# Feed-forward weights at earlier steps of the last body, quantising between the gated products, and three products and the last conversion's third chunk on GpSimd

## The chip, the cores and the metric

One core of one Trainium2 chip runs the kernel. The metric is the device time of one execution in microseconds, the median over several runs. The engines are TensorE (PE, with its weight loads as PEld), VectorE (DVE), ScalarE (ACT), GpSimd (POOL) and SyncE (SP, which here only issues DMAs). They run their own instruction streams in order and meet through semaphores.

## What is computed

```
x   32 x 64 x 128 latents, ctx 32 x 1601 x 128, mask 32 x 1601
x = x + cross_attention(ctx, layernorm(x), mask)    # 16 heads of 64, softmax over 1601 + 64 keys, layernorm of the output
x = x + self_attention(layernorm(x))                # 16 heads of 8, with slopes * (key - query)
x = x + ffn(layernorm(x))
ffn(x):  xq = fake_quant(x, clip_x)                 # one scale: sigmoid(clip) * max|x| / 127 over the whole tensor
         h  = silu(xq @ q(w_gate).T) * (xq @ q(w_up).T)          # 352 wide; q(w): per row scale max|w| / 127, rounded
         return fake_quant(h, clip_down) @ q(w_down).T           # again one scale over the whole tensor
```

The kernel looks at the mask (whether any of the first 1201 keys is in play) and runs one of two plans, over all 1601 context keys or over the last 400. The run profiled here takes the second, WINDOW.

## The kernel before, in words

**Bodies and steps.** The 32 batches go in 16 pairs. A body is one pair: 16 steps, eight for each of its two batches (k = 0, 1; t = s % 8). Body 0 and 1 are written out, 2 to 14 are a hardware loop, body 15 is the last. In a step TensorE makes a tile of scores (three f16 products of 512 columns), ScalarE takes the exponential twice (L1084 as f16, L1075 as f32), GpSimd subtracts the one from the other (L845, `low_probs`), and TensorE multiplies high and low parts with the values two steps later (L1421, `values`). Other work is hung on steps by a table: a pair's own tail starts in its body and goes on in the next (`background`, with s + 16). The tables name the step: ST1, YN, ST2 are the output product of the cross attention with the division by the denominators, M0/P0/X1 its layernorm, M1/P1/XH the next layernorm, XHT a transpose, QKV the self attention's projections, KEXP the keys spread over heads by a mask (GpSimd, L905), VBLK the values, SC the scores (L1516), ALIBI and SMAX slopes and maximum (VectorE), SHIFT, EXP, PT, PV, CX (context divided, VectorE L1858, L1860), CXT, WO, X2/P2, XF the normalised input of the feed-forward part. Within a step each engine does its own work in the order: attention, tail of the pair, feed-forward weights.

**Feed-forward weights** (`ffn_weights`, in body 15 only, for k = 1 and by t). SP loads them early in the body (`load_ffn`, L689 to L691). VectorE finds the scales (L1743 to L1750), rounds each of three chunks of gate, of up, and the down weights with three instructions (L1707, L1708, L1709, each waiting for the one before), and makes a diagonal of the down scales (L1758). TensorE transposes them into two banks (L1285, L1289, L1292), and VectorE copies them out (L1763 to L1768).

**The drain.** Behind body 15 stand the last two value tiles, then `drain_pairs`: the tails of pair 14 (table BEFORE_LAST) and 15 (LAST_PAIR) side by side, 22 steps. At step 0 GpSimd spreads the keys of pair 14, TensorE makes its scores, then for pair 15 the sum of denominators (L1462) and the output product (L1480, L1490). VectorE takes ALIBI and SMAX of pair 14, then the reciprocals of pair 15's denominators (L1873) and the products with them (L1882).

**The feed-forward part.** After the largest |x| is known, four groups of 512 tokens are quantised: raised by a constant (L2010 on VectorE for groups 0, 1; L1200 on ScalarE for 2, 3), then L2013 and L2014 on VectorE. Then 12 products, m = 3 * group + chunk: TensorE makes gate and up into banks (L1615, L1616), ScalarE SiLU into one of two buffers (L1207), VectorE up times SiLU (L2029), and behind each group the largest |h| (L2022, in the last group in two pieces). Then the scale of h through TensorE (L1619, L1621), and for four groups j: h to int8, all three chunks (L2044); int8 to bf16, chunks 0 and 1 on ScalarE (L1211), chunk 2 on VectorE (L2046); 12 products (L1628); scaling (L2052) and the residual added, on GpSimd for j = 0, 1 (L966), on VectorE for 2, 3 (L2055); a DMA out.

## Time and profile before

| | us |
|---|---|
| median of 3 runs (848.68 to 850.6) | 848.82 |
| the profiled execution | 846.89 |
| its span | 845.1 |
| busy: PE, DVE, ACT, POOL | 762.6, 606.2, 586.6, 519.2 |
| granted TensorE clock, mean | 0.964 of full |

The span is what the profile's times refer to, from its start. In the 40 slices of the page (21 us each) PE shows 9 tenths in slices 5 to 36 and then 7, 7, 4, 3 (the last four: 7743), with a granted clock of 9 tenths up to slice 37 and then 6, 6, 5. The page's chain that ended last has 65% on PE, 18% on DVE, 6% issue, 5% ACT, 2% POOL.

### The profile page before, as it was taken

Reading aid. Unit: us, or ns where it says so; the run is one execution under the profiler, and the core shown is the slowest. Engines: PE = TensorE matmul, PEld = TensorE weight load, DVE = VectorE, ACT = ScalarE, POOL = GpSimd, SP = SyncE. Lnnn points to the kernel's source line nnn. Section 1 sums busy time; section 2 is a strip of 40 time slices with the busy share of each in tenths; the row PEclk is TensorE's granted clock in tenths of the full one; section 3 lists DMA queues with packets and bytes.
Section 4 is the critical chain, followed back from the end, with each engine's and each line's share of the span. In section 5 each row is a group of like instructions: output and inputs, shape, how many; then the busy total and the mean of one; then the engine's idle time right before and its main releaser. Section 6 shows DMA issues by size and latency. Waiting matters only on the chain.

```text
span 845.1 us, 22525 instructions
## 1 busy us (share of the span) xinstructions
PE 762.6 (90%) x7062; PEld 419.5 (50%) x7063; DVE 606.2 (72%) x1515; ACT 586.6 (69%) x1018; POOL 519.2 (61%) x660
## 2 busy tenths in 40 slices
PE   5698999999999999999999999999999999997743
PEld 3343544545464555545454545555455546455412
DVE  5777676676768686876777686878767676757587
ACT  5487677868777676868686776768686867673242
POOL 3366676766767676666667676757666676764101
PEclk9799999999999999999999999999999999999665
DMA  6212222121212212021212121121112121200001
GB/s 191 56 44 79 74 66 50 46 69 39 59 53 55 57 53 56 21 55 43 68 41 66 43 57 55 53 59 32 44 41 68 43 68 38 73 14 17 4 0 50
DMA packets 95821, 44.42 MB, mean 53 GB/s; under 512 B 66500, under 2 KB 87848, under 8 KB 95656
## 3 DMA queue, kind: packets, MB, share of 16 engines
q1 hardware_dynamic: 95728, 43.93, 18.9%
q8 instruction: 17, 0.28, 0.1%
q14 instruction: 20, 0.16, 0.1%
q10 hardware_dynamic: 56, 0.05, 0.0%
HBM read 24.20 MB, written 3.34 MB: 33 GB/s over the span
## 4 chain that ended last, share of the span: by engine, by line
PE 65%; DVE 18%; issue 6%; ACT 5%; DVEq 2%; POOL 2%; DMA 1%; ACTq 0%; SPq 0%; POOLq 0%
PE bank L1421 14%; PE bank L1480 7%; PE bank L1384 6%; PE bank L1339 5%; PE bank L1388 5%; PE bank L1386 5%; PE bank L1356 4%; PE bank L1497 3%; PE bank L1541 3%; DVE xf_all L1851 3%; DVE mx L1822 3%; PE bank L1526 2%; PE bank L1516 2%; PE bank L1355 2%; DVE st L1779 1%
## 5 line engine op out<-in xcount | busy, mean ns | idle before, releaser
L845 POOL TENSOR_TENSOR p<-arena,p 128x512 f16<-128x512 f32 x256 | 297.1, 1161 | 167.2 <-ACT arena L1075 166.7
L1084 ACT ACTIVATE p<-bank,maskbias 128x512 f16<-128x512 f32 x224 | 155.1, 692 | 125.6 <-PE bank L1388 124.6
L1421 PE MATMUL bank<-p,xv 128*128 128x512 f16 (+1 forms) x768 | 182.6, 380 | 4.1 <-POOL p L845 2.7
L1822 DVE TENSOR_REDUCE mx<-bank 128x1 f32<-128x464 f32 x256 | 154.1, 634 | 32.3 <-PE bank L1356 31.0
L1075 ACT ACTIVATE arena<-bank,maskbias 128x512 f32<-128x512 f32 x224 | 154.6, 690 | 0.5 <-POOL p L845 0.5
L1818 DVE TENSOR_TENSOR qkl_l<-bank,qkl_h 128x512 f16<-128x512 f32 x64 | 41.1, 686 | 71.2 <-ACT qkl_h L1064 71.1
L1421 PEld LDWEIGHTS bank<-p,xv 128*128 128x128 f16 (+1 forms) x768 | 57.2, 97 | 70.0 <-issue 22.6
L1384 PE MATMUL bank<-qkc_h,xtT_h 128*128 128x512 f16 (+1 forms) x256 | 86.9, 389 | 0.0
L1388 PE MATMUL bank<-qkc_h,xtT_l 128*128 128x512 f16 (+1 forms) x256 | 85.0, 379 | 0.0
L1386 PE MATMUL bank<-qkc_l,xtT_h 128*128 128x512 f16 (+1 forms) x256 | 85.0, 379 | 0.0
L1356 PE MATMUL bank<-xtT_h,qkc_h 128*128 128x400 f16 x256 | 79.7, 338 | 0.0
L1480 PE MATMUL bank<-arena,wvF 128*64 128x128 f32 x1024 | 69.3, 278 | 0.0
L1339 PE MATMUL bank<-arena,wk_h 64*128 64x128 f16 x1024 | 50.1, 217 | 15.5 <-DVE arena L1809 14.9
L1480 PEld LDWEIGHTS bank<-arena,wvF 128*64 128x64 f32 x1024 | 54.7, 136 | 14.5 <-issue 13.1
L1814 DVE SCALAR_TENSOR_TENSOR arena<-bank,ident,arena 128x512 f16<-128x512 f32 x60 | 42.0, 738 | 26.6 <-ACT arena L1061 26.6
L1339 PEld LDWEIGHTS bank<-arena,wk_h 64*128 64x128 f16 x1024 | 37.0, 94 | 42.1 <-DVE arena L1809 22.1
L1355 PE MATMUL bank<-ltT,qkl_h 128*128 128x64 f16 x256 | 50.7, 198 | 4.9 <-DVE qkl_l L1818 3.2
L1355 PEld LDWEIGHTS bank<-ltT,qkl_h 128*128 128x128 f16 x256 | 24.9, 97 | 59.0 <-DVE mx L1822 26.3
L1788 DVE TENSOR_SCALAR raw<-raw,mv,rstd 128x128 f32<-128x128 f32 x128 | 51.1, 458 | 1.9 <-POOL rstd L854 1.7
L1061 ACT ACTIVATE arena<-bank,ident 128x512 f16<-128x512 f32 x60 | 37.9, 684 | 16.3 <-PE bank L1339 16.3
L1339 PE MATMUL bank<-arena,wk_l 64*128 64x128 f16 x512 | 46.1, 216 | 0.0
L1084 ACT ACTIVATE p<-bank,zrow 128x512 f16<-128x512 f32 x32 | 22.0, 687 | 26.5 <-PE bank L1392 26.5
(267 smaller groups left out, 1548.8 us busy)
## 6 DMA issues: line engine op xcount, KB each, us to landing
arena<-den_dram SPq DMA_DIRECT2D x62, 128.0 KB, 3.2
qkc_h<-arena SPq DMA_DIRECT2D x30, 256.0 KB, 2.4
qkc_l<-arena SPq DMA_DIRECT2D x30, 256.0 KB, 2.5
raw<-in_ctx SPq DMA_DIRECT2D x32, 192.0 KB, 2.4
lt<-lt_dram SPq DMA_DIRECT2D x60, 32.0 KB, 2.1
arena<-in_L_xattn_Wkv SPq DMA_DIRECT2D x1, 1024.0 KB, 6.8
raw<-in_ctx SPq DMA_DIRECT2D x64, 8.0 KB, 2.0
ltT_dram<-x_all SPq DMA_DIRECT2D x4, 256.0 KB, 3.0
```

What stands on the lines that cost most here:

```text
L845: g.tensor_tensor(p_halves[0:r, slot, 1, :], p_all[0:r, (plan.halves_made(0, k, t) - 1) % 2, :], p_halves[0:r, slot, 0, :], ALU.subtract). ...
L1075: a.activation(p_all[0:r, (plan.halves_made(0, k, t) - 1) % 2, :], sbank[t % SRING][0:r, :], ACT.Exp, bias=bias).then_inc(s_probs_ready, 1)
L1084: a.activation(p_halves[0:r, slot, 0, :], sbank[t % SRING][0:r, :], ACT.Exp, bias=bias)
L1339: op = mm(by_batch(both[odd])[:, :, to], w[rws, cl, c, :], q[rws, c, :].rearrange("p (k t) -> p k t", k=2), start=first, stop=final)
L1355: mm(bk[:, rest:rest + M], qkl_h[:, par, col], ltT[:, par, 0, :], start=True, stop=True)
L1356: op = mm(bk[:, 0:rest], qkc_h[:, par, col], xtT_h[:, par, 512 * part:plan.KEYS], start=True, stop=True)
L1384: op = mm(dst, keys_h, q_h[:, col], start=True, stop=False)
L1386: op = mm(dst, keys_h, q_l[:, col], start=False, stop=False)
L1388: op = mm(dst, keys_l, q_h[:, col], start=False, stop=tile > 0)
L1421: op = mm(bk[:, :], halves_of[at, row, :], p_halves[at, slot, prob, :], start=tile < 2 and n == 0, stop=last and n == 2)
L1480: op = mm((one, two)[q // 2][E * odd:E * odd + E, (c % 4) * P:(c % 4) * P + P], wvF[:, cl, head:head + E], z[:, :, col:col + M], start=cl ...
L1822: v.tensor_reduce(mx[:, hq_tile, part:part + 1], bk[:, 0:width], AX.X, ALU.max).then_inc(s_jobs_taken, 1)
```

## The change

- The feed-forward weights go by the step s of the body, not by t within k = 1: scales at s = 7 (before 10), rounding at 8 and 9 (11, 12), TensorE's transposes and the copies at 10, 11, 12, 13 (12, 13, 14, 15).
- For WINDOW the keys of pair 14 are spread before the last `low_probs`, and its scores are made between the last two value tiles.
- Group 1 is raised on ScalarE. Groups 0 and 1 are quantised before the products, group 2 behind product 2, group 3 behind product 5. The maximum of a group comes behind the first product of the next.
- Products 1, 4 and 7 are made on GpSimd: ScalarE writes SiLU and, scaled, up into SBUF buffers of their own.
- The cast of chunk 2 to bf16 is on GpSimd, in front of its two residual additions.

```diff
--- before.py
+++ after.py
@@ -53,7 +53,7 @@
...
 ALIBI_AT = 16
-FFN = dict(scales=2, round=[3, 4], fw=[4, 5], fwd=[6], wd=[7])
+FFN = dict(scales=7, round=[8, 9], fw=[10, 11], fwd=[12], wd=[13])
 
@@ -201,7 +201,7 @@
...
 BEFORE_LAST = Drain(False, dict(
-    NEVER, KEXP=0, X1B=1, SC=0, ALIBI=[1, 1], SMAX=1, SHIFT=2, EXP=2, PT=[5, 5], PT_OUT=[5, 5], PV=6, CX=8, CXT=9, CXT_OUT=9, WO=10, X2=11, P2=12, XF=14))
+    NEVER, X1B=1, SC=-2, ALIBI=[1, 1], SMAX=1, SHIFT=2, EXP=2, PT=[5, 5], PT_OUT=[5, 5], PV=6, CX=8, CXT=9, CXT_OUT=9, WO=10, X2=11, P2=12, XF=14))
 LAST_PAIR = Drain(True, dict(
@@ -348,6 +348,8 @@
...
         s_xqT_ready = es.enter_context(nc.semaphore("xqT_ready"))
+        s_up_copied = es.enter_context(nc.semaphore("up_copied"))
+        s_h_pool = es.enter_context(nc.semaphore("h_pool"))
         s_xtT_hi = es.enter_context(nc.semaphore("xtT_hi"))
@@ -444,6 +446,7 @@
...
         h8 = words(12288, 1536).bitcast(I8).rearrange("p (c t) -> p c t", c=3)
+        pool_sil, pool_up = (raw[:, :, :, :].rearrange("p a c d -> p (a c d)")[:, at:at + 512] for at in (2048, 2560))
         yout = raw[:, :, :, :].rearrange("p a c d -> p (a c d)")[:, 0:2048].rearrange("p (a b) -> p a b", a=4)
@@ -597,6 +600,16 @@
...
 
+        POOL_TILES = (1, 4, 7)
+
+        def on_pool(m):
+
+            return sum(n <= m for n in POOL_TILES)
+
+        def on_dve(m):
+
+            return m + 1 - on_pool(m)
+
         block = es.enter_context(nc.Block())
@@ -879,6 +892,14 @@
...
 
+            def spread_keys(p):
+
+                pool.wait_ge(s_qk_ready, p + 1)
+                if happened(2 * p):
+                    pool.wait_ge(s_self_scores, 2 * p)
+                g.tensor_tensor(kexp, kT[:, :].rearrange("p (k m) -> p k m", k=2).unsqueeze(2).to_broadcast([P, 2, AH // 2, M]),
+                                halfmask[:, :].unsqueeze(1).unsqueeze(3).to_broadcast([P, 2, AH // 2, M]), ALU.mult).then_inc(s_kexp_ready, 1)
+
             def tail(plan, p, s):
@@ -899,11 +920,7 @@
...
                 if s == at["KEXP"] and not plan.own:
-                    pool.wait_ge(s_qk_ready, p + 1)
-                    if happened(2 * p):
-                        pool.wait_ge(s_self_scores, 2 * p)
-                    g.tensor_tensor(kexp, kT[:, :].rearrange("p (k m) -> p k m", k=2).unsqueeze(2).to_broadcast([P, 2, AH // 2, M]),
-                                    halfmask[:, :].unsqueeze(1).unsqueeze(3).to_broadcast([P, 2, AH // 2, M]), ALU.mult).then_inc(s_kexp_ready, 1)
+                    spread_keys(p)
                 if s == at["SHIFT"]:
@@ -950,6 +967,8 @@
...
                 body(PAIRS - 1, 2, True)
+                if plan is WINDOW:
+                    spread_keys(PAIRS - 2)
                 low_probs(plan, PAIRS - 1, 1, plan.STEPS - 1)
@@ -961,6 +980,13 @@
...
             drain_pairs(None, tail, 14, DRAIN_STEPS)
+            for m in POOL_TILES:
+                pool.wait_ge(s_up_copied, on_pool(m))
+                g.tensor_tensor(hT[:, m % 3, 512 * (m // 3):512 * (m // 3) + 512], pool_up, pool_sil, ALU.mult).then_inc(s_h_pool, 1)
+            for j in range(4):
+                pool.wait_ge(s_h8_ready, j + 1)
+                part = slice(512 * j, 512 * j + 512)
+                g.tensor_copy(hq[:, 2, part], h8[:, 2, part]).then_inc(s_hq_ready, 1)
             for j in range(2):
@@ -1196,15 +1222,24 @@
...
             act.wait_ge(s_xscale_ready, 1)
-            for m in (2, 3):
-                a.activation(xq32[:, 512 * m:512 * m + 512], abank[m - 2][:, :], ACT.Identity, scale=fst[:, 3:4], bias=magic[:, :]).then_inc(s_x_raised, 1)
+            for m in (1, 2, 3):
+                act.wait_ge(s_groups_out, 2)
+                src = xfT[:, 512:1024] if m == 1 else abank[m - 2][:, :]
+                a.activation(xq32[:, 512 * m:512 * m + 512], src, ACT.Identity, scale=fst[:, 3:4], bias=magic[:, :]).then_inc(s_x_raised, 1)
             act.wait_ge(s_sgu_ready, 1)
...
                 act.wait_ge(s_gate_made, m + 1)
-                if happened(m - 1):
-                    act.wait_ge(s_h_ready, m - 1)
-                a.activation(sil[:, m % 2, :], bank[2 + m % 3][:, :], ACT.Silu, scale=sgu[:, 0, c:c + 1]).then_inc(s_silu_ready, 1)
+                if m in POOL_TILES:
+                    if on_pool(m) > 1:
+                        act.wait_ge(s_h_pool, on_pool(m) - 1)
+                    a.activation(pool_sil, bank[2 + m % 3][:, :], ACT.Silu, scale=sgu[:, 0, c:c + 1]).then_inc(s_silu_ready, 1)
+                    act.wait_ge(s_up_made, m + 1)
+                    a.activation(pool_up, up_bank[m % 3][:, :], ACT.Identity, scale=sgu[:, 1, c:c + 1]).then_inc(s_up_copied, 1)
+                else:
+                    if on_dve(m) > 2:
+                        act.wait_ge(s_h_ready, on_dve(m) - 2)
+                    a.activation(sil[:, on_dve(m) % 2, :], bank[2 + m % 3][:, :], ACT.Silu, scale=sgu[:, 0, c:c + 1]).then_inc(s_silu_ready, 1)
             for j in range(4):
@@ -1572,8 +1607,8 @@
...
                             late_weights(s + 2 * plan.STEPS * since, since)
-                        if last and k == 1:
-                            ffn_weights(plan, t)
+                        if last:
+                            ffn_weights(plan, s - plan.STEPS + WINDOW.STEPS)
 
@@ -1583,6 +1618,8 @@
...
                     values(plan, PAIRS - 1, 1, t)
+                    if plan is WINDOW and t == plan.STEPS - LAG:
+                        drained(BEFORE_LAST, PAIRS - 2, BEFORE_LAST.at["SC"])
 
@@ -1610,8 +1647,10 @@
...
                     pe.wait_ge(s_silu_ready, m - 2)
-                if happened(m - 2):
-                    pe.wait_ge(s_h_ready, m - 2)
+                if m - 3 in POOL_TILES:
+                    pe.wait_ge(s_up_copied, on_pool(m - 3))
+                elif m >= 3:
+                    pe.wait_ge(s_h_ready, on_dve(m - 3))
                 mm(bank[2 + m % 3][:, :], fwT[:, 0, rows], xqT[:, 512 * tg:512 * tg + 512], start=True, stop=True).then_inc(s_gate_made, 1)
@@ -1976,8 +2015,8 @@
...
                             late_weights(s + 2 * plan.STEPS * since)
-                        if last and k == 1:
-                            ffn_weights(t)
+                        if last:
+                            ffn_weights(s - plan.STEPS + WINDOW.STEPS)
 
@@ -2004,31 +2043,39 @@
...
             dve.wait_ge(s_groups_out, 2)
-            for m in range(4):
+
+            def quantised(m):
+
                 part = slice(512 * m, 512 * m + 512)
-                if m < 2:
+                if m == 0:
                     link(v.tensor_scalar(xq32[:, part], xfT[:, part], fst[:, 3:4], MAGIC, ALU.mult, ALU.add))
                 else:
-                    dve.wait_ge(s_x_raised, m - 1)
+                    dve.wait_ge(s_x_raised, m)
                 link(v.tensor_scalar(xqT[:, part], xq32[:, part], MAGIC, QMAX, ALU.subtract, ALU.min))
                 v.tensor_scalar(xqT[:, part], xqT[:, part], -QMAX - 1.0, None, ALU.max).then_inc(s_xqT_ready, 1)
-                if m == 0:
-                    v.tensor_scalar(sgu[:, :, :], fw_s[:, :, :], fst[:, 2:3], None, ALU.mult).then_inc(s_sgu_ready, 1)
+
+            quantised(0)
+            v.tensor_scalar(sgu[:, :, :], fw_s[:, :, :], fst[:, 2:3], None, ALU.mult).then_inc(s_sgu_ready, 1)
+            quantised(1)
             dve.wait_ge(s_sgu_ready, 1)
...
 
-                dve.wait_ge(s_h_ready, 3 * tg + c1)
+                dve.wait_ge(s_h_ready, on_dve(3 * tg + c1 - 1))
+                if on_pool(3 * tg + c1 - 1):
+                    dve.wait_ge(s_h_pool, on_pool(3 * tg + c1 - 1))
                 return v.tensor_reduce(hmax[:, 3 * tg + c0:3 * tg + c1], hT[:, c0:c1, 512 * tg:512 * tg + 512], AX.X, ALU.max, apply_absolute_value=True)
 
-            for m in range(12):
+            for m in (m for m in range(12) if m not in POOL_TILES):
                 tg, c = divmod(m, 3)
...
                 dve.wait_ge(s_silu_ready, m + 1)
-                v.scalar_tensor_tensor(h, up_bank[m % 3][:, :], sgu[:, 1, c:c + 1], sil[:, m % 2, :], ALU.mult, ALU.mult).then_inc(s_h_ready, 1)
-                if tg < 3 and c == 2:
-                    largest(tg, 0, 3)
+                v.scalar_tensor_tensor(h, up_bank[m % 3][:, :], sgu[:, 1, c:c + 1], sil[:, on_dve(m) % 2, :], ALU.mult, ALU.mult).then_inc(s_h_ready, 1)
+                if tg < 2 and c == 2:
+                    quantised(tg + 2)
+                if tg > 0 and c == 0:
+                    largest(tg - 1, 0, 3)
                 if tg == 3 and c >= 1:
@@ -2042,8 +2089,6 @@
...
                 v.tensor_scalar(h8[:, :, part], hT[:, :, part], fst[:, 7:8], None, ALU.mult).then_inc(s_h8_ready, 1)
-                dve.wait_ge(s_h8_ready, j + 1)
-                v.tensor_copy(hq[:, 2, part], h8[:, 2, part]).then_inc(s_hq_ready, 1)
                 if j == 0:
```

## Rows read from the trace of the kernel before

**Rows 1.** Timeline of VectorE in the last body: start, duration, engine, line, operation, shapes, idle before.
```profile
745.15 0.67 DVE L1882 TENSOR_TENSOR arena<-bank,arena 128x512 f32<-128x512 f32 x1
...
749.93 0.30 DVE L1846 BATCH_NORM_STATS2 sst<-bank 128x6 f32<-128x128 f32 x1 [4.11 <-PE bank L1497]
...
752.30 0.06 DVE L1743 MEMSET fw_s<- 128x6 f32 x1
...
754.25 0.12 DVE L1750 RECIPROCAL fwd_s<-fwd_s 128x1 f32<-128x1 f32 x1
...
757.93 1.11 DVE L1709 TENSOR_SCALAR fwq<-arena 128x128 bf16<-128x128 f32 x1
...
758.97 0.27 DVE L1707 TENSOR_SCALAR arena<-arena,fw_i 96x128 f32<-96x128 f32 x1
...
765.00 0.28 DVE L1758 TENSOR_SCALAR arena<-ident,fwd_s 128x128 f32<-128x128 f32 x1
```

**Rows 2.** Waits from 755 to 765 us: who waited for whom, us, times, longest.
```profile
PE bank L1285 <- DVE fwq L1709: 3.5, 2, 2.3
```

**Rows 3.** Timeline of SP's DMA queue, 728 to 746 us.
```profile
734.96 0.42 SPq L691 DMA_DIRECT2D arena<-in_L_ffn_w_down  x1
```

**Rows 4.** DMA issues by line, 728 to 746 us: count, KB, median us to landing.
```profile
arena<-in_L_ffn_w_down SPq DMA_DIRECT2D x1, 176.0 KB, 2.4
```

**Rows 5.** Timelines of VectorE and GpSimd, earlier in the last body.
```profile
723.09 1.96 DVE L1788 TENSOR_SCALAR raw<-raw,mv,rstd 128x128 f32<-128x128 f32 x4
...
723.67 1.30 POOL L845 TENSOR_TENSOR p<-arena,p 128x512 f16<-128x512 f32 x1 [0.37 <-ACT arena L1075]
...
738.70 0.68 DVE L1921 SCALAR_TENSOR_TENSOR arena<-bank,alibi 128x512 f32<-128x512 f32 x1
```

**Rows 6.** Timeline of GpSimd in the last body.
```profile
747.43 1.16 POOL L845 TENSOR_TENSOR p<-arena,p 128x512 f16<-128x512 f32 x1
...
748.96 1.17 POOL L845 TENSOR_TENSOR p<-arena,p 128x512 f16<-128x512 f32 x1
...
752.53 1.15 POOL L845 TENSOR_TENSOR p<-arena,p 128x512 f16<-128x512 f32 x1 [1.15 <-ACT arena L1075]
...
769.11 1.15 POOL L845 TENSOR_TENSOR p<-arena,p 128x512 f16<-128x512 f32 x1 [0.67 <-ACT arena L1075]
```

**Rows 7.** Timelines of GpSimd, VectorE and TensorE in the drain.
```profile
770.22 1.90 POOL L905 TENSOR_TENSOR arena<-kT,halfmask 128x1024 f32<-128x1024 f32 x1
...
775.80 1.75 DVE L1873 RECIPROCAL arena<-bank 128x256 f32<-128x256 f32 x1
...
780.92 1.16 PE L1490 MATMUL bank<-wout_sb,arena 128*128 128x128 f32 x8 [0.32 <-DVE arena L1882]
```

**Rows 8.** Instructions on the arena, VectorE: count, duration ns min/median/max, start, form.
```profile
L2022 DVE TENSOR_REDUCE hmax<-arena x5: 686/1753/1755, 813.7 to 826.9; 128x3 f32<-128x1536 f32 x3, 128x2 f32<-128x1024 f32 x1, 128x1 f32<-128x512 f32 x1
...
L2013 DVE TENSOR_SCALAR arena<-arena x4: 419/424/427, 808.0 to 810.7; 128x512 bf16<-128x512 f32 x4
```

**Rows 9.** Timeline of the gated products.
```profile
809.59 1.48 ACT L1207 ACTIVATE arena<-bank,sgu 128x512 f32<-128x512 f32 x2 [0.60 <-remote]
...
811.32 1.40 DVE L2029 SCALAR_TENSOR_TENSOR arena<-bank,sgu,arena 128x512 f32<-128x512 f32 x2
```

**Rows 10.** Timeline of the last conversion and the output.
```profile
829.67 1.28 DVE L2044 TENSOR_SCALAR arena<-arena,fst 128x1536 int8<-128x1536 f32 x1
...
830.99 0.43 DVE L2046 CAST arena<-arena 128x512 bf16<-128x512 int8 x1
...
839.86 1.04 DVE L2055 TENSOR_TENSOR raw<-raw,x_all 128x512 f32<-128x512 f32 x1
```

**Rows 11.** Lines L873 and L966 of GpSimd: count, duration ns min/median/max.
```profile
L873 POOL CAST xv<-raw x32: 602/608/612, 28.1 to 732.4; 128x508 f16<-128x508 f32 x32
...
L966 POOL TENSOR_TENSOR raw<-raw,x_all x2: 1266/1502/1737, 837.4 to 838.6; 128x512 f32<-128x512 f32 x2
```

**Rows 12.** Windows: us, busy us of PE, PEld, DVE, ACT, POOL, granted clock, DMA share, GB/s.
```profile
788.00:790.00 2.00, 1.63 (x11) 1.01 (x7) 1.85 (x6) 0.46 (x2) 0.00 (x0) 0.50 0.00 0
```

## The prediction

> **What bounds the kernel now.** I read the page's slices first: TensorE is busy nine tenths up to the last three of forty, so only what TensorE waits for counts there, and behind the loop every engine's chain counts. Then the chain of waits from 700 us on, then the timeline of each engine over it. The reader is to see four stretches.
> The last body ends badly: VectorE idles 4.1 us before 749.93, then makes the feed-forward weights from 752.30 to 765.28 [rows 1], and TensorE stands 3.5 us for them [rows 2]. In the drain the chain runs through VectorE: scores of pair 14, their maximum, the reciprocals at 775.80 [rows 7]. In the gated products VectorE is busy nearly throughout (products 0.70 us in a row, the maximum of a group 1.75) [rows 8, 9]. In the last conversion it alternates 1.28 and 0.43 us [rows 10].
>
> **A. Weights made earlier.** Before: scales at step 10, rounding at 11 and 12. After: scales at 7, rounding at 8 and 9, TensorE's transposes at 10, 11, 12, 13. Nothing is added or taken away. The last weight transfer is issued at 734.96 [rows 3] and takes 2.4 us [rows 4]; VectorE comes to step 7's end at 745.80, so the load is no wait, and SP's order is the same.
> What matters is how GpSimd and VectorE exclude each other [rows 5]. Four normalisations (0.33 each alone) take 1.96 us, because a GpSimd subtraction came in between them; that subtraction itself took 1.30 instead of 1.16, since it waited for one of the four. So one waits for the other's instruction, and they alternate. The instruction at 738.70, with one input in PSUM, ran its usual 0.68 beside a subtraction of 738.74 to 739.90. The rounding is of the first kind: 0.23 alone, 1.11 under GpSimd [rows 1].
> The walk: scales 745.80 to 747.87 (2.07, from 752.30 to 754.37). A chunk's three instructions take 0.79 alone (758.97 to 759.76 in the chain), three chunks 2.4. At 747.87 GpSimd is in a subtraction until 748.59, then has an addition and another subtraction [rows 6]: VectorE's first instruction waits to 748.55, its second to 749.2, its third to 750.55, and the rest end at 752.35. Behind them stands the moments step that ran at 749.93; it now ends at 752.9. For it waits GpSimd (two small instructions, 0.85), and behind those the subtraction of 752.53, now at 754.0 to 755.1: TensorE needs it at about 756.5, so this is covered.
> Second round: 2.4, with the down weights and the diagonal 1.3 (763.94 to 765.28), and two subtractions between, 2.1 in all: 752.95 to 758.7. Behind it stand X1 and its moments (1.35), a copy (0.3) and the self context CX (0.55): CX is ready at 761.0. TensorE, no longer held for the weights, is at the transpose of CX at 759.0 and waits 2.0 to 2.1; the second transposes wait 0.2. Removed 3.5, added 2.3: **-1.2 us**. Ends: with no rounding blocked, CX is 4.1 earlier and the whole 3.5 is gained (-3.5); with two or three more blocked, at 0.9 each, +1.0 and more.
>
> **B. Spread keys and self scores of pair 14 ahead.** GpSimd makes the spread keys (1.90) before the last subtraction instead of behind it [rows 7]; its wait is for the keys' copy by ScalarE at step 14, which is there. It had 0.67 idle before that subtraction [rows 6], so the subtraction, TensorE's last values and ScalarE's copies of them come 1.2 later against the rest, but the self scores now fill TensorE's hole. The sum of denominators, which used to start behind keys and scores, keeps its place (minus A). VectorE's scores and maximum are over before it, so the reciprocals of 775.80 start with the denominators, 0.7 earlier. TensorE then no longer waits 0.32 at 780.92. **-0.3 us**; ends -0.8 (all of VectorE's) and +0.8 (the last subtraction's delay, if it is not hidden).
>
> **C. Gated products.** Raising group 1 moves from VectorE (0.48) to ScalarE (0.70, in the place where it was idle until 809.59): SiLU 0 starts 0.1 later. Quantising groups 2 and 3 (0.43 and 0.29 each, 0.74 with the waits) moves from in front of product 0 to behind products 2 and 5. Products 1, 4, 7 leave VectorE (2.1), and ScalarE gets three copies of up (0.70 each). On GpSimd a product is one of 1.16 to 1.27 [rows 5, 11].
> The walk: SiLU 0 ends 810.4, product 0 at 811.2. ScalarE then does SiLU 1, the copy of up 1, SiLU 2, to 812.6, and VectorE is idle 1.4. From there it has 8 products (5.6), two quantisations (1.5), three maxima of 1.68 and those of 1.17 and 0.72, which is 14.05: 826.65. GpSimd's products fall at 811.9, 814.7 and 818.0, the quantisations at 813.4 and 817.2: no overlap. Each product of GpSimd is over more than 1.5 us before the maximum that waits for it. ScalarE's fifteen are 10.5 in 16, TensorE at half clock 0.86 a step: neither is late. Before it was 827.6. **-0.9 us**; ends -2.3 (no hole) and +0.5 (a quantisation behind a product of GpSimd, 1.2, and the next SiLU with it).
>
> **D. Last conversion.** Removed: four casts of 0.43 on VectorE [rows 10]. Added: four on GpSimd. No row shows int8 to bf16 there; f32 to f16 of 508 columns is 0.61 [rows 11]. Take 0.6; ends 0.43 and 1.2. With t from 829.67: VectorE's h8 0 ends 1.28, the row for the scales 1.5. Now GpSimd reads and writes SBUF while VectorE wants it. h8 handles 1536 columns in 1.28 us, 0.83 ns each, as fast as only the kind that was blocked above: 512 columns in 0.42 [rows 8]; the maximum over 1536 takes 1.75, 1.1 ns each, and that kind was never blocked. So I take it as blocked. GpSimd's cast 0 gets 1.5 to 2.1; h8 1 2.1 to 3.3 and h8 2, already queued, to 4.5; cast 1 to 5.1; h8 3 to 6.3; casts 2 and 3 to 7.4. TensorE needs ScalarE's and GpSimd's part: its four blocks (1.44, 1.29 in a row) start 2.45, 5.1, 6.9, 8.2 and end 9.6. GpSimd's additions now start behind its casts, at 7.4, 1.26 each, to 9.95; VectorE's addition 2, two SBUF inputs, waits for them (such a wait is in the 1.04 of 839.86), ends 10.5, then scaling 3 and addition 3 to 11.8. Before, 840.90 is 11.2. **+0.6 us**. If VectorE's h8 always wins the order, the same GpSimd additions end at 9.95 again, so the sum is the same. Ends: without exclusion -1.8 (below), with casts of 1.2, +2.3.
> The Trainium skill, "SBUF — State Buffer", section "Who interferes with whom", says that a cast or tensor_scalar in a 2-port mode and a GpSimd instruction shut each other out for the whole instruction, and that the one issued first goes first. By it D is +0.6; if it did not hold for this form, -1.8. No row has GpSimd beside h8.
>
> **Sum.** -1.2 - 0.3 - 0.9 + 0.6 = -1.8. The profiled execution is 846.89 (span 845.1 and 1.8 around it), so it gives 845.1. The median of the runs shown, 848.82, lies 1.9 above that execution, and I forecast in its terms: **847.0 us**. 0.3% is 2.5 us, about what a measurement of this kernel can tell from no change.
>
> **Rivals.**
> 1. GpSimd's cast does not shut out h8. Then h8 ends at 5.2, TensorE at 8.0, VectorE at 9.4: D is -1.8 and the time **844.6**. For it: no row of this pair. Against it: the rate of h8. Chance 0.15.
> 2. The weights vanish from the path: GpSimd's subtractions fall beside VectorE's scales and PSUM instructions, CX comes before 759, A is -3.3: **844.9**. For it: 4.1 us of idle VectorE. Against: GpSimd is busy from 747.43 to 750.1 nearly without a gap [rows 6]. Chance 0.17.
> 3. Slower: the rounding stands in front of moments, X1 and CX, and GpSimd's queue stands behind those. It decides from CX at 761.0 on: each us later is one more for TensorE. Four more blocked instructions (0.9 to 1.1, 4.3 in all) put CX at 765.3; A is +3.1, B still -0.3, C -0.9, D +0.6: **851.3**. For it: three of seven chunks were blocked by about 0.9 before. Against: GpSimd has but four subtractions under the whole stretch, and the walk has them all. Chance 0.11.
> 4. The clock. TensorE's granted clock is 0.50 of full from 788 on [rows 12], that is 1.2 instead of 2.4 GHz, after a stretch in which TensorE had short holes. If it falls some 3 us earlier against the work, about 1.5 us of matmuls take twice as long: **848.5**. Chance 0.12.
>
> **Chances.** The forecast 0.45. Its own spread puts 0.06 below -2.5 and 0.01 above +2.5. Faster: 0.15 + 0.17 + 0.06 = 0.38; slower 0.11 + 0.01 = 0.12; same 0.50. The range takes in rivals 1, 2 and 4 and the ends of B and C: 844.4 to 849.6. Left out are rival 3, and the cases in which rivals 1 and 2 come together.
>
> **What would show it.** In the profile after: A, the waits of TensorE for the rounded weights gone, and one of about 2 us for CX in their place; rounding instructions of over 1 us between 748 and 758. B, spread keys in front of the last subtraction, no wait of TensorE for VectorE before the second half of the output product. C, VectorE idle about 1.4 us behind product 0 and not after. D, h8 instructions of 1.7 to 1.9 us in place of 1.28, or GpSimd casts that long; the last addition of VectorE behind GpSimd's. It is wrong if h8 keeps 1.28 beside casts of 0.6, or if TensorE has no wait for CX.

## The result, and the profile after

The changed kernel takes **840.39 us** (median of 4 runs, 839.63 to 840.75); the kernel before took 849.71 beside it (4 runs, 848.68 to 851.55). The ratio is 0.9891, with an interval of 0.9877 to 0.9905: 9.3 us less where 1.8 were forecast, and outside the range. The profiled execution is 840.75, its span 838.9, against 846.89 and 845.1. So 6.1 us lie between the two profiled executions and 9.3 between the medians, and both differences have to be explained.

The page of the changed kernel, against the table of before:

```profile
PE 762.7 (91%) x7063; PEld 420.9 (50%) x7063; DVE 604.0 (72%) x1507; ACT 589.4 (70%) x1022; POOL 527.3 (63%) x667
...
PE   5598999999999999999999999999999999998763
...
PEclk9699999999999999999999999999999999999855
```

TensorE is as busy as before (762.7 against 762.6), GpSimd has 8 us more. The last four slices are 8763 where they were 7743, and the clock has 8 tenths in slice 38, where it had 6, and then 5 and 5 for 6 and 5: the same work, closer together.

**The last body.** VectorE's timeline, where rows 1 had the weights behind 752.30 (everything starts 1.27 later in this execution: the last body's SMAX stands at 745.29, in the trace of before at 744.02):

```profile
749.14 0.81 DVE L1746 TENSOR_SCALAR arena<-arena,fw_i 128x128 f32<-128x128 f32 x1
749.98 0.38 DVE L1747 TENSOR_SCALAR arena<-arena 128x128 f32<-128x128 f32 x1
750.39 1.09 DVE L1748 TENSOR_SCALAR fwq<-arena 128x128 bf16<-128x128 f32 x1
751.40 0.28 DVE L1746 TENSOR_SCALAR arena<-arena,fw_i 128x128 f32<-128x128 f32 x1
...
752.83 0.29 DVE L1885 BATCH_NORM_STATS2 sst<-bank 128x6 f32<-128x128 f32 x1
...
754.29 1.18 DVE L1747 TENSOR_SCALAR arena<-arena 128x128 f32<-128x128 f32 x1
...
757.16 1.18 DVE L1748 TENSOR_SCALAR fwdq<-arena 128x352 bf16<-128x352 f32 x1
...
760.30 0.29 DVE L1899 TENSOR_TENSOR cx<-bank,sden 128x128 f32<-128x128 f32 x1
```

The first rounding instruction starts at 749.14, which is 747.87 in before's time, to the hundredth as walked. Five instructions are blocked by a subtraction of GpSimd (0.81, 0.38, 1.09, 1.18, 1.18). CX is over at 760.59, or 759.3 in before's time; the walk said 761.0. The waits of TensorE from 755 to 765 us, where rows 2 had 3.5 us for the weights:

```profile
PE bank L1580 <- DVE cx L1899: 0.5, 1, 0.5
...
PE bank L1456 <- POOL p L858: 0.2, 1, 0.2
```

**The gated products**, VectorE's timeline (rows 9 before):

```profile
807.34 0.75 DVE L2074 SCALAR_TENSOR_TENSOR arena<-bank,sgu,arena 128x512 f32<-128x512 f32 x1 [0.85 <-ACT arena L1242]
809.26 0.75 DVE L2074 SCALAR_TENSOR_TENSOR arena<-bank,sgu,arena 128x512 f32<-128x512 f32 x1 [1.17 <-ACT arena L1242]
809.92 0.42 DVE L2054 TENSOR_SCALAR arena<-arena 128x512 bf16<-128x512 f32 x1
...
811.25 1.74 DVE L2067 TENSOR_REDUCE hmax<-arena 128x3 f32<-128x1536 f32 x1
```

Product 0 is over 3.9 behind the reciprocal of 804.21, as walked; then the one hole, 1.17 where 1.4 was expected, and none over 0.2 after it.

**The last conversion** (rows 10 before). GpSimd's and TensorE's timelines, and of VectorE the line of h8 by its instructions (durations ns min/median/max):

```profile
826.56 0.61 POOL L989 CAST arena<-arena 128x512 bf16<-128x512 int8 x1 [11.13 <-DVE arena L2091]
828.31 2.99 POOL L989 CAST arena<-arena 128x512 bf16<-128x512 int8 x3 [1.14 <-DVE arena L2091]
831.29 2.50 POOL L992 TENSOR_TENSOR raw<-raw,x_all 128x512 f32<-128x512 f32 x2
...
829.48 4.00 PE L1667 MATMUL bank<-fwdT,arena 128*128 128x128 bf16 x36 [0.32 <-POOL arena L989]
```
```profile
L2091 DVE TENSOR_SCALAR arena<-arena,fst x4: 1265/1274/1530, 825.2 to 829.4; 128x1536 int8<-128x1536 f32 x4
```
```profile
832.97 1.37 DVE L2100 TENSOR_TENSOR raw<-raw,x_all 128x512 f32<-128x512 f32 x1
...
834.97 0.69 DVE L2100 TENSOR_TENSOR raw<-raw,x_all 128x512 f32<-128x512 f32 x1
```

One h8 of four is longer, by 0.25; two casts of four are longer, by 0.45. Neither waits for the whole of the other. The traces of d_only and fill_down (below) have the same lengths in the same places: 1.53 for one h8, 1.06 for two casts. From the first h8, the last block of TensorE ends at 8.3 (walked 9.6), GpSimd's casts at 6.1 (7.4), its additions at 8.6 (9.95), VectorE at 10.45 (11.8; before 11.2). The order of events is the one forecast, each step 1.3 earlier.

### The profile page after: what moved, and what is told of

It is laid out like the page before. It is cut to its first block, busy times and chain, and to the rows that moved or that the text cites. A ratio compares the mean times of both kernels' runs of the same rounds, so it can differ in the third digit from the quotient of the medians.

```text
span 838.9 us, 22529 instructions
## 1 busy us (share of the span) xinstructions
PE 762.7 (91%) x7063; PEld 420.9 (50%) x7063; DVE 604.0 (72%) x1507; ACT 589.4 (70%) x1022; POOL 527.3 (63%) x667
## 4 chain that ended last, share of the span: by engine, by line
PE 66%; DVE 17%; issue 7%; ACT 5%; POOL 2%; DVEq 2%; DMA 1%; ACTq 0%; SPq 0%; POOLq 0%
PE bank L1456 14%; PE bank L1515 8%; PE bank L1419 6%; PE bank L1374 5%; PE bank L1423 5%; PE bank L1421 5%; PE bank L1391 4%; PE bank L1532 3%; PE bank L1576 3%; DVE xf_all L1890 3%; DVE mx L1861 3%; PE bank L1551 2%; PE bank L1561 2%; PE bank L1390 2%; DVE st L1818 1%
## 5 line engine op out<-in xcount | busy, mean ns | idle before, releaser
L1087 ACT ACTIVATE arena<-bank,ident 128x512 f16<-128x512 f32 x60 | 38.0, 684 | 15.8 <-PE bank L1374 15.8
L1118 ACT ACTIVATE arena<-bank 128x512 f32<-128x512 f32 x64 | 38.5, 601 | 3.2 <-PE bank L1456 3.2
```

## The experiments

All in one table. Four stretches are read from VectorE's timeline, as differences of start times: **S1** from SMAX in the last body to the first reciprocal of the drain (line 1873 of before); **S2** to the largest |x|; **S3** from the reciprocal of x's scale to the largest |h|; **S4** from the first h8 to the end of the span. "Low until 783" lists when, in the profiled execution, the granted clock was 0.50 for 3.4 us, and "low from" is where it fell for the first long stretch (10 us and more). Medians and ratios are of all executions of a run, the stretches and the clock of its profiled one.

| run | median (lowest to highest, runs) | ratio, interval | S1 | S2 | S3 | S4 | low until 783 | low from |
|---|---|---|---|---|---|---|---|---|
| before | 846.89 (the profiled execution alone) | | 31.78 | 29.53 | 20.35 | 15.48 | none | 787.7 |
| control | 849.36 (848.29 to 851.48, 12) | 1.0005 [0.9996, 1.0014] | 33.39 | 30.05 | 20.35 | 14.48 | 765.5 | 789.4 |
| a_only | 843.56 (842.98 to 844.35, 6) | 0.9935 [0.9923, 0.9948] | 29.17 | 29.40 | 20.34 | 14.50 | none | 785.3 |
| b_only | 845.48 (844.26 to 848.93, 10) | 0.9961 [0.9949, 0.9974] | 31.97 | 29.25 | 20.34 | 14.47 | 763.6 | 787.5 |
| c_only | 847.39 (846.03 to 848.75, 12) | 0.9976 [0.9968, 0.9985] | 34.53 | 30.97 | 18.71 | 14.51 | 764.5, 774.8 | 788.4 |
| d_only | 848.76 (845.54 to 850.57, 12) | 0.9986 [0.9973, 0.9998] | 34.49 | 31.01 | 20.35 | 13.72 | 764.5, 774.7 | 788.4 |
| ab_only | 843.69 (842.77 to 845.02, 6) | 0.9927 [0.9913, 0.9942] | 28.73 | 30.25 | 20.35 | 14.47 | none | 783.5 |
| no_b | 841.51 (840.99 to 843.01, 6) | 0.9905 [0.9891, 0.9920] | 29.16 | 29.28 | 18.96 | 13.69 | none | 786.0 |
| no_d | 843.77 (840.58 to 844.87, 6) | 0.9928 [0.9911, 0.9944] | 28.72 | 28.20 | 18.97 | 14.48 | none | 789.0 |
| after | 840.39 (839.63 to 840.75, 4) | 0.9891 [0.9877, 0.9905] | 28.74 | 28.23 | 18.97 | 13.72 | none | 790.0 |
| after_again | 840.34 (839.52 to 841.20, 5) | 0.9895 [0.9880, 0.9909] | 28.73 | 27.58 | 18.97 | 13.72 | none | 793.1 |
| fill_w | 845.36 (843.31 to 850.75, 7) | 0.9951 [0.9938, 0.9965] | 32.88 | 31.95 | 20.35 | 14.47 | 773.8 | 787.4 |
| fill_both | 847.16 (845.40 to 849.42, 12) | 0.9964 [0.9950, 0.9979] | 31.76 | 29.36 | 20.34 | 14.49 | none | 788.1 |
| c_front | 847.11 (843.59 to 849.28, 10) | 0.9956 [0.9936, 0.9976] | 34.52 | 30.88 | 17.50 | 14.51 | 765.5, 775.7 | 789.4 |
| fill_ffn | 840.27 (840.00 to 841.45, 5) | 0.9894 [0.9880, 0.9909] | 28.73 | 29.49 | 18.90 | 13.70 | none | 785.6 |
| fill_all | 840.07 (839.97 to 840.96, 5) | 0.9895 [0.9881, 0.9909] | 28.74 | 28.29 | 18.91 | 13.70 | none | 785.7 |
| fill_down | 840.75 (838.72 to 841.72, 6) | 0.9887 [0.9863, 0.9912] | 28.71 | 29.24 | 18.93 | 12.88 | none | 784.5 |
| fill_down_order | 842.23 (840.46 to 842.87, 6) | 0.9900 [0.9876, 0.9925] | 28.71 | 30.66 | 18.91 | 13.71 | none | 783.7 |
| quant_front | 839.88 (837.94 to 840.67, 4) | 0.9881 [0.9862, 0.9899] | 28.72 | 30.31 | 17.51 | 13.72 | none | 783.6 |
| quant_front_fill | 838.53 (838.22 to 840.28, 4) | 0.9877 [0.9860, 0.9893] | 28.72 | 28.11 | 18.03 | 12.85 | none | 790.0 |

### The parts by themselves, and the kernel before again

Control is the kernel before, unchanged. The other three have one part of the diff each.

```diff
# a_only: part A
-FFN = dict(scales=2, round=[3, 4], fw=[4, 5], fwd=[6], wd=[7])
+FFN = dict(scales=7, round=[8, 9], fw=[10, 11], fwd=[12], wd=[13])
# b_only: part B
-    NEVER, KEXP=0, X1B=1, SC=0, ...
+    NEVER, X1B=1, SC=-2, ...
+                    spread_keys(PAIRS - 2)
# c_only: part C
+        POOL_TILES = (1, 4, 7)
+                if tg < 2 and c == 2:
+                    quantised(tg + 2)
```

Expected of control:

> The kernel before, unchanged. Two theories of why the medians differ by 9.3 us while the two profiled executions differ by 6.2. Theory 1: the profiled execution of before (846.9) is just a lucky one, in which the granted clock fell late; then other executions of it have a lower mean clock than 0.964, and the profile of this run, if it is near 849.7, shows the fall to 0.50 well before 787 us. Theory 2: executions of before are slower for another reason (more waits in the loop); then the mean clock is 0.964 and the extra 3 us stand before 700 us.

Expected of a_only:

> Only the weights made at earlier steps (part A). Theory 1, the walk with its sizes: TensorE's 3.5 us of waits for the weights are replaced by a wait of 0.5 for CX, so the last values come 2.7 us earlier and the time falls by 2.5 to 3. Theory 2, the clock: the gain is larger, 4 to 6 us, because with fewer holes in the last body the granted clock stays at 1.00 for longer; then the profile shows its fall later against the work of the drain. My prediction had -1.2 for this part.

Expected of b_only:

> Only the spread keys and self scores of pair 14 ahead (part B). Theory 1, the walk: about -0.3 us, at most -0.8. Theory 2, the clock: the order of TensorE's work around its hole of 1 to 2 us decides when the clock falls; then it is -1 to -3 us, with no wait in the profile that is shorter by as much.

Expected of c_only:

> Only the feed-forward stage's products and quantisation (part C), everything before it as in the kernel before. Theory 1: -1.4 us, as between the two profiles from the reciprocal of the x scale to the maximum of h (20.3 to 19.0 us). Theory 2: the gain needs the clock's rise in the stage; then the time in the stage differs by over 0.5 us between executions with their clock. Nothing before the stage may change.

Control is at 849.36 like the other runs of before, so the median stands, but its profile is not that of before. TensorE's timeline has the same hole (a stretch in which it stands still) for the weights as rows 2; the windows behind it differ. First control, then before (columns as in rows 12):

```profile
764.88 0.32 PE L1285 MATMUL bank<-identb,fwq 128*128 128x128 bf16 x3 [2.31 <-DVE fwq L1709]
```
```profile
766.00:768.00 2.00, 2.00 (x8) 1.26 (x6) 1.17 (x6) 1.26 (x2) 0.54 (x1) 0.50 0.00 0
```
```profile
766.00:768.00 2.00, 2.00 (x19) 1.12 (x18) 1.32 (x8) 1.29 (x4) 1.41 (x3) 1.00 0.00 0
```

It was granted 0.50 of full behind the hole (1.2 GHz) and 1.00 (2.4 GHz) without the fall. The two windows hold partly different matmuls, so their counts (8 and 19) don't compare; the same three value products right behind the hole do, in control and then in before:

```profile
765.88 1.48 PE L1421 MATMUL bank<-p,xv 128*128 128x512 f16 x3
```
```profile
764.97 0.81 PE L1421 MATMUL bank<-p,xv 128*128 128x512 f16 x3
```

c_only shows what that does to single matmuls of 512 columns, 0.63 for 0.38, and a second fall behind the next holes:

```profile
764.45 0.40 PE L1310 MATMUL bank<-identb,fwq 128*128 128x128 bf16 x3 [2.32 <-DVE fwq L1736]
764.66 0.63 PE L1409 MATMUL bank<-qkc_h,xtT_h 128*128 128x512 f16 x1
...
768.88 0.38 PE L1409 MATMUL bank<-qkc_h,xtT_h 128*128 128x512 f16 x1
...
772.27 0.82 PE L1446 MATMUL bank<-p,xv 128*128 128x512 f16 x3 [1.07 <-POOL p L858]
774.18 1.45 PE L1541 MATMUL bank<-arena,qT 64*64 64x512 f32 x8 [1.08 <-issue]
775.56 2.80 PE L1487 MATMUL bank<-arena,sel 128*64 128x512 f32 x6
```

S1 orders the runs that keep the order of before by the number of such falls: none, 31.78; one, 33.39; two, 34.5. A fall costs S1 1.1 to 1.6 us. The mean clock of the twelve executions of control is 0.954 to 0.958; that of the profiled execution of before is 0.964. So the profiled execution was one without these falls, and by their mean clocks most are not. Of the five traces that keep this order and this hole (before, control, c_only, d_only, c_front) four show the fall behind it.

**S2** goes by the clock too. No run but fill_all changes its work, and yet it lies between 27.6 and 31.95. What orders it is how long after the first reciprocal of the drain the clock falls for the long stretch: 9.2 to 10.5 us (fill_w, d_only, c_only, c_front, fill_down_order, quant_front, ab_only) give 31.95 down to 30.25; 11.3 in control gives 30.05; 11.9 to 12.3 (before, fill_ffn, fill_both, a_only, no_b, fill_down, b_only) give 29.5 to 29.2; 15.8 to 16.0 (quant_front_fill, no_d, after) give 28.1 to 28.2; 19.2 in after_again gives 27.58. The one exception, fill_all, has the clock back at 1.00 from 796.0 to 799.4.

**A** alone takes S1 from 31.78 to 29.17, which is 2.6, and the median down by 5.5 (0.0065 of 849.7). The 2.9 between them is about what the falls cost: its profile has none before 785. It has none although TensorE still waits 1.29 and 1.08 us around the last value tile, so a hole of this size is followed by a fall in some executions and not in others; what decides it is open. **B** alone takes 1.4 from S1 against control, both with one fall; its median is 3.3 lower. **C** alone takes 1.64 from S3 and 2.0 from the median.

### Two parts, and all but one

```diff
# ab_only: the diffs of a_only and b_only together
# no_b: the changed kernel with SC and KEXP of before
-    NEVER, X1B=1, SC=-2, ...
+    NEVER, KEXP=0, X1B=1, SC=0, ...
# no_d: the changed kernel with the casts on VectorE; d_only: before with them on GpSimd
-                g.tensor_copy(hq[:, 2, part], h8[:, 2, part]).then_inc(s_hq_ready, 1)
+                dve.wait_ge(s_h8_ready, j + 1)
+                v.tensor_copy(hq[:, 2, part], h8[:, 2, part]).then_inc(s_hq_ready, 1)
# after_again: the changed kernel, unchanged
```

Expected of ab_only:

> Parts A and B together, feed-forward stage as before. If both gain by their own waits (2.7 and 0.4 us) and share what they save of the clock, the sum is less than 5.5 + 3.3: theory 1 (shared clock) gives -6 to -7 us; theory 2 (independent gains) gives -8.8. The profile should show no fall of the clock before 785.

Expected of no_b:

> The changed kernel with part B undone: keys spread behind the last subtraction, scores of pair 14 at step 0 of the drain. Theory 1: with A in place B is worth its waits alone, 0.4 to 0.8 us, so 0.4 to 0.8 slower than the changed kernel. Theory 2: B is worth 3.3 us as it was alone.

Expected of no_d:

> The changed kernel with part D undone: the casts of chunk 2 back on VectorE. My prediction had D at +0.6 (this run 0.6 faster than the changed kernel); by the profile of the changed kernel the stretch from the first h8 to the last addition is 10.45 us against 11.23, and the output's transfers start earlier by 1.0: this run 0.8 to 1.7 us slower than the changed kernel.

Expected of after_again:

> The changed kernel once more, for more executions beside those of its variants. It should lie at 840.4 with a mean clock of 0.965 to 0.971. If some of its executions show 0.961, as four of six of the run without part D did, these will lie 2 to 4 us higher: then D has no part in that difference.

Expected of d_only:

> Only the last conversion (part D). From the first h8 to the end of the span the seven profiles without D have 14.5 us (one has 15.5), the two with it 13.7: so 0.8 us faster than before. My prediction had +0.6. If the run without D (3.4 slower than the changed kernel by the medians) is to be believed instead, this one is 3 us faster.

With A in place **B** is worth 0.44 in S1 (29.17 to 28.73, and 29.16 to 28.74 from the other side), not 1.4, and 1.1 in the median of no_b against the changed kernel. The waits of TensorE between the last body and the sum of denominators tell the two cases apart. First a_only, then the changed kernel:

```profile
767.74 0.82 PE L1421 MATMUL bank<-p,xv 128*128 128x512 f16 x3 [1.29 <-POOL p L845]
769.64 1.09 PE L1516 MATMUL bank<-arena,qT 64*64 64x512 f32 x8 [1.08 <-issue]
```
```profile
769.22 1.09 PE L1551 MATMUL bank<-arena,qT 64*64 64x512 f32 x8 [1.51 <-POOL arena L900]
...
772.05 1.94 PE L1497 MATMUL bank<-arena,sel 128*64 128x512 f32 x8 [0.89 <-ACT arena L1118]
```

They add up to 2.37 and 2.40: with A, TensorE is early enough to wait for the spread keys themselves. Without A they are 2.15 in control (1.07 and 1.08) and 1.16 in b_only (0.27 and 0.89). What is left of B in both cases is VectorE's maximum, which no longer stands between the sum of denominators and the reciprocals: these start 1.98 behind the start of the sum in the changed kernel and 1.97 in b_only, for 2.56 in a_only and 2.55 in control.

**D** is worth 0.76 in S4 from either side (14.48 to 13.72 in no_d against after, and in control against d_only). d_only's median, 1.2 below before, agrees. no_d's does not: 3.4 above after_again. Its six executions lie in two groups, 840.58 and 841.67 at a mean clock of 0.966 and 0.967, and 843.2 to 844.9 at 0.959 to 0.961; the profiled one is of the first. None of the five executions of after_again is below 0.967. Why a cast at the end should go with a lower clock is open, since only one execution has a trace.

The parts don't add up by medians (5.5 + 3.3 + 2.0 + 1.2 = 12.0, against 9.3): A and B each take falls of the clock away, and these can go only once. By stretches they do, if B is counted on top of A: S1, S3 and S4 of the changed kernel are those of ab_only, no_b and d_only to within 0.02. Only C alone is off, with 18.71 in S3 for 18.97; product 6 waits there for TensorE's product of up, which took 0.38 in c_only, at a granted clock of 1.00, and 0.63 in the changed kernel, where it was 0.50 from 813.9 on.

### The holes filled

The same product of TensorE, unused, is put into its waits. Nothing is taken away, and what TensorE waits for doesn't come earlier.

```diff
# fill_w: the kernel before; fill_both: with the last two lines too, four each in front of and
# behind the second of the last value tiles
                     if kind == "fw":
+                        for _ in range((5, 10)[k]):
+                            mm(bk[:, :], wq_h[:, 0:P], wq_h[:, 0:HALF], start=True, stop=True)
                         pe.wait_ge(s_fwq_ready, 1 + k)
...
+                        pe.wait_ge(s_ffn_done, 3)
+                        filler(jbank[0], 4)
```

Expected of fill_w:

> The kernel before, with 5 and 10 extra products of 512 columns on TensorE (1.1 and 2.2 us at full clock) in front of its two waits for the rounded weights; the waits of 1.2 and 2.3 us stay, only they are not idle. The products go to the bank that the transposes then overwrite. Theory 1, the clock follows TensorE's holes: the fall to 0.50 that control shows at 765.5 us is gone, and the time falls by 1.5 to 2 us although work was added. Theory 2, the clock does not depend on these holes: no change, or up to 0.3 us slower, and the fall at 765 stays.

Expected of fill_both:

> The kernel before, with extra products of TensorE in its two waits for the weights, as before, and eight more behind the last body, in the wait in front of the last value tile. Theory: the time of the usual execution of the kernel before, 849.7, is its work plus two falls of the granted clock to 0.50 for 3.4 us, one behind the hole for the weights and one behind the hole of the last values; with both holes filled it is 843.5 to 845.5, every execution at a mean clock of 0.966 or more, and none near 850. From the maximum of pair 14's scores to the first reciprocal it keeps some 32 us, since nothing of VectorE's order is changed. Rival: the second fall is not from that hole; then as with the first hole alone, 845.4 in the median and single executions of 848 to 851.

fill_w does 15 products more than before and is **4.2 us faster** (ratio 0.9951, interval clear of 1). The work and its order are the same but for the added products, and the mean clock is 0.966 to 0.968 in six of the seven executions, for 0.956 to 0.959 in those of before beside them: the clock behind the hole costs time. Its profiled execution is its slowest, 850.75, and shows that the gain is not in every one: with the first hole filled, the next one gives a fall. TensorE's timeline, and a window behind it:

```profile
771.61 0.82 PE L1423 MATMUL bank<-p,xv 128*128 128x512 f16 x3 [1.07 <-POOL p L845]
773.51 1.77 PE L1518 MATMUL bank<-arena,qT 64*64 64x512 f32 x8 [1.08 <-issue]
```
```profile
774.00:777.00 3.00, 3.00 (x14) 0.56 (x8) 1.68 (x3) 0.00 (x0) 0.46 (x1) 0.50 0.00 0
```

In fill_both the same waits are 0.21 and 0.17 and the window has the full clock:

```profile
770.58 0.82 PE L1423 MATMUL bank<-p,xv 128*128 128x512 f16 x3 [0.21 <-POOL p L845]
772.43 1.09 PE L1523 MATMUL bank<-arena,qT 64*64 64x512 f32 x8 [0.17 <-POOL arena L905]
```
```profile
774.00:777.00 3.00, 3.00 (x42) 2.14 (x40) 2.97 (x4) 0.00 (x0) 1.05 (x2) 1.00 0.02 5
```

Its profiled execution, 845.93 with S1 at 31.76, is the profiled execution of before without its late output: there the span ends 4.2 behind VectorE's last instruction (840.90), in control 3.25 (843.75 to 847.0), and 846.89 less 1.0 is 845.9. But my theory's number failed. The median is 847.16, not 843.5 to 845.5, and no better than fill_w's (the intervals overlap); five of twelve executions still have a clock of 0.958 to 0.962 and take 846.2 to 849.4. The holes explain most of the distance between 845.9 and 849.7, not all of it: where the remaining falls sit isn't known, the place of the long fall in S2 was left to chance, and what the eight further products cost by themselves wasn't measured.

### Part C taken apart

```diff
# c_front: c_only with the quantising in front; quant_front: the same in the changed kernel
             quantised(1)
+            quantised(2)
+            quantised(3)
...
-                if tg < 2 and c == 2:
-                    quantised(tg + 2)
```

Expected of c_front:

> The kernel before with part C alone, but groups 2 and 3 quantised in front of product 0, as before. If VectorE bounds the stretch, the two quantisations (0.74 each with their waits) come in front of product 0 again, where TensorE and ScalarE have work to get ahead with: the hole of 1.17 behind product 0 shrinks, and of the 1.5 in front only what the hole does not give back is lost, 0.3 to 1.5, so from the scale of x to the last maximum of h 19.0 to 20.2 instead of 18.7 with C whole and 20.35 without it. Rival: the interleaving alone carries C, and the three products on GpSimd give nothing: 20.2 to 20.4.

Expected of quant_front:

> The changed kernel with one part of its change taken back: groups 2 and 3 are quantised in front of product 0, not behind products 2 and 5. Theory: in front, the two quantisations cost 0.4, since VectorE waits 0.85 there for the first SiLU anyway, and behind products they cost 0.66 each on the engine that bounds; so from the scale of x to the last maximum of h it is 17.7 instead of 18.97, and the time 839.1. Rival: with the weights earlier and the cast on GpSimd the stretch is bounded otherwise than in the run with part C alone: 18.5 to 19.0, and 840.3 as before.

Both sides of c_front's expectation missed. S3 is 17.50, below c_only's 18.71: what ScalarE and GpSimd take over (the raising of group 1, the copies, the three products) and the later maxima give 2.85 together (from 20.35), and quantising between the products **costs 1.2**. VectorE's timeline of c_only, then of c_front:

```profile
814.87 0.75 DVE L2061 SCALAR_TENSOR_TENSOR arena<-bank,sgu,arena 128x512 f32<-128x512 f32 x1 [0.85 <-ACT arena L1232]
816.79 0.75 DVE L2061 SCALAR_TENSOR_TENSOR arena<-bank,sgu,arena 128x512 f32<-128x512 f32 x1 [1.17 <-ACT arena L1232]
```
```profile
816.00 0.74 DVE L2063 SCALAR_TENSOR_TENSOR arena<-bank,sgu,arena 128x512 f32<-128x512 f32 x1
817.53 1.51 DVE L2063 SCALAR_TENSOR_TENSOR arena<-bank,sgu,arena 128x512 f32<-128x512 f32 x2 [0.80 <-ACT arena L1232]
```

In c_only VectorE idles 0.85 in front of product 0 and 1.17 behind it, in c_front only 0.80 behind it. In front, the two quantisations (0.66 each, 1.32 together) fill 1.22 of idle time; between the products, where VectorE has no gap, they fill none. quant_front repeats it in the changed kernel, where it costs 1.5 (18.97 to 17.51). Its median is 0.5 under after_again, not 1.2; in its profile the clock falls at 783.6 already, and S2 is 30.31 against 28.23 and 27.58.

### The clock in the feed-forward part

```diff
# fill_ffn, on the changed kernel
+            filler(bank[3], 3)                  # in front of the products
+                    filler(abank[1], 1)         # in front of each product from the fourth on
+            filler(abank[1], 8)                 # while the largest |h| is found
+            filler(abank[1], 5)                 # behind it
# fill_all: as fill_ffn, and six more in three waits of the drain
# fill_down: as fill_ffn, with 17 and 11 for 8 and 5
# fill_down_order: as fill_down, VectorE's scalings 2 and 3 ahead of its additions 2 and 3
# quant_front_fill: fill_down with the quantising in front
```

Expected of fill_ffn:

> The changed kernel with extra products on TensorE where it waits in the feed-forward stage: 3 in front of the first product, 1 in front of each from product 3, 8 before the maximum of h, 5 before the last conversion's blocks. Theory 1, the clock follows the holes here too: it stands at 1.00 in the last conversion, its four blocks take 0.7 instead of 1.3 us, and the time falls by 1 to 2 us. Theory 2: the clock stays at 0.50; then the extra products are in the way and the time is 0 to 1 us longer.

Expected of fill_all:

> The same, and with extra products in the drain: 2 before the second transposes of probabilities, 1 before the transpose of the context, 3 before the last transpose of the normalised input. Theory 1: the clock also rises before 810, and another 1 to 2 us go. Theory 2: no rise, 0.3 to 1.5 us slower than the changed kernel.

Expected of fill_down:

> The changed kernel with more extra products in TensorE's waits of the feed-forward part: one behind each of the products from the fourth on, 17 while the maximum of h is found, 11 in front of the last conversion's products. Theory: the granted clock is 1.00 in the last conversion too, its blocks take 0.7 us instead of 1.3, and from the first h8 to the end it is 12.8 to 13.2 instead of 13.7, the time 839.5. Rival: the clock is still 0.50 there, or VectorE and GpSimd set the end anyway, and the time is that of the changed kernel, 840.3, or up to 1 more.

Expected of fill_down_order:

> As the run before it, and VectorE scales chunks 2 and 3 before it adds chunks 2 and 3, so that its first addition does not hold up the last scaling behind GpSimd's additions. Theory: the last addition comes 0.2 to 0.5 earlier than without this, whatever the clock does. Rival: addition 2 waits for GpSimd as before and nothing stood behind it that mattered: no difference, within 0.1 in the profile.

Expected of quant_front_fill:

> The run before this with the extra products of TensorE in its waits of the feed-forward part, by which the granted clock was 1.00 in the last conversion. Theory: the two gains add up: 17.7 for the stretch of the gated products, 12.9 from the first h8 to the end, 838.0 in the median. Rival: what the clock gives there is lost in single executions, as in fill_down, whose median was no better than the changed kernel: 839 to 840.

fill_ffn and fill_all hold the clock at 1.00 from 809.4 to 823.1, and it moves S3 by 0.07, with the added products in TensorE's way: VectorE bounds nearly all of it (product 6, above, was the one that waited for the clock). The last conversion is at 0.50 again in both, and the time is that of the changed kernel. fill_all's products in the drain did bring the clock back, to 1.00 from 796.0 to 799.4, and its S2 is 28.29 where fill_ffn, with the fall at the same place, has 29.49; its median is only 0.2 lower, and the intervals overlap. fill_down holds the clock at 1.00 in the last conversion too:

```profile
810.00:835.00 25.00, 14.75 (x98) 7.21 (x96) 22.36 (x29) 9.94 (x13) 8.89 (x8) 1.00 0.11 31
```
```profile
828.34 0.85 PE L1679 MATMUL bank<-fwdT,arena 128*128 128x128 bf16 x12 [0.91 <-POOL arena L989]
829.53 0.84 PE L1679 MATMUL bank<-fwdT,arena 128*128 128x128 bf16 x12 [0.34 <-POOL arena L989]
```

A block takes 0.85, where three took 4.00 in the changed kernel, S4 is 12.88 for 13.72, and the two small products in front give 0.3. Of that 1.1 the median shows nothing (840.75); S2 alone differs by more between profiled executions than this gives. fill_down_order was to bring the last addition forward by 0.2 to 0.5 and didn't: VectorE ends 9.7 behind the first h8 for 9.6, and since both of its outputs now leave at the very end, S4 is 13.71, 0.8 worse than without it. In quant_front_fill S4 is 12.85 as hoped, but S3 is 18.03 and not 17.7: the added products cost 0.5 of the 1.5 that quantising in front gives. It has the lowest median, 838.53, with a ratio of 0.9877 against 0.9895 for after_again; the intervals overlap, so a version that beats the changed kernel by some 1.5 us is likely and not shown.

## Why the prediction was wrong

**The base.** This is the largest miss. "The median of the runs shown, 848.82, lies 1.9 above that execution, and I forecast in its terms": I carried the 1.9 as a constant. Most of it was falls of the clock behind holes that the change takes away: the traces of control and a_only and the gain of fill_w show them, though fill_both leaves part of the distance open. An execution of before without falls and without its late output is 845.9; the usual one is 849.7. These 3.8 of the 9.3 stood in no term of the sum. Rival 4 had the mechanism, but only as a loss, and only for the fall at 788.

Taken from control's profiled execution (848.83) instead, the way to 840.75 is 8.1: the last body starts 0.55 later, S1 is 4.65 shorter (3.0 of it against an execution without a fall), S2 1.8, S3 1.4, S4 0.8. The 1.8 of S2 is work that nobody changed, with the clock falling 16.0 us behind the first reciprocal in place of 11.3.

**The sum** in stretches is A -2.6, B -0.4, C -1.4, D -0.8, together -5.2 where -1.8 was forecast. 845.9 less 5.2 is 840.7, and the profiled execution after is 840.75. (Its body starts 1.27 later and S2 is 1.30 shorter, which cancel. That they do is luck: S2 is shorter because the clock fell later, 16.0 us behind the reciprocal for 11.9.)

- **A: -2.6 for -1.2.** The step that failed is the walk's "CX is ready at 761.0": it came at 759.3. Five instructions were blocked by 3.3 in all, where the walk had about 4: the first round ended 0.8 earlier than in it, the moments took 0.1 less, the second round 0.6 less, and what stands between it and CX 0.2 less. TensorE, expected to wait 2.0 to 2.1, waited 0.47 and then 0.17. That leaves 2.9 of the 3.5; 0.2 of it goes into a longer wait for the last value tile (1.29 for 1.07 in a_only). It lies nearer to rival 2 (-3.3) than to the forecast, but not by its mechanism: GpSimd's subtractions did fall into the rounding, and cost less.
- **B: -0.4 for -0.3.** Right, given A, and by the step that was walked, the reciprocals starting with the denominators (0.6 for 0.7). Alone it is -1.4: without A the scores also fill a hole of TensorE that A moves.
- **C: -1.4 for -0.9.** The mechanism was right to the place of the one hole (1.17 for 1.4); the walk from there was 13.89 for 14.05. The walk moved the two quantisations from in front of product 0 to between the products without asking what each place costs: left in front, the stretch is 1.2 to 1.5 shorter.
- **D: -0.8 for +0.6.** The step "I take it as blocked" was half right, and its price was wrong: I took a blocked instruction to wait for the whole of the other, so that the casts would end at 7.4, and they ended at 6.1. Measured, one h8 beside a cast is longer by 0.25 and two casts beside h8 by 0.45, which is part of the other's length; how the two share that time isn't shown. Rival 1 (no exclusion, -1.8) comes close up to TensorE's end, 8.0 for 8.3, and then fails by something else: it left out that VectorE's addition 2 waits for GpSimd's additions, which the forecast had, and which made it 1.37 for 0.69.
  The section of the Trainium skill that I cited ("SBUF — State Buffer", "Who interferes with whom") says that the one shuts the other out for the whole instruction. For the rounding instructions the trace agrees (1.18 for 0.23). For h8 and the cast it doesn't, and the measurement decides: a cast ran from 828.31 to 829.38 inside an h8 of 828.17 to 829.44 that took its usual 1.27.

The slower rival, CX at 765.3, was 6 us from the truth.

## What to carry to other kernels

Before you forecast from a profiled execution, ask why it is not at the median. If the mean granted clock of the other executions is lower, look for holes of TensorE in front of work that it is bound by: a change that closes such a hole can give back the hole and then the half clock behind it, here 2.6 and about as much again. Filling the hole with unused products is a cheap way to test this. And work that can run while the bounding engine waits should stay in that wait: moved "between" other work it is on the path.
